# Attention: GpSimd adds layer 0's product to the residual behind its first product of values, and VectorE's statistics follow the score products

## The reference, cut to what matters

```python
x = L0_attn_x
xn = _layernorm(x)
s = _L0_attn_ref(xn, ...)            # recurrence over the tokens, output product, gate, residual
g = _silu(_L0_ffn_ref(xn, ...))
x = x + s * g                        # the add that the change moves
xn = _layernorm(x)                   # its mean and variance are "the statistics"
s = _L1_attn_ref(xn, ...)            # for each position i of dimension 1: a 4 x 4 attention in 16 heads of 16
g = _silu(_L1_ffn_ref(xn, ...))      # mixture of 8 experts
x = x + s * g

# _L1_attn_ref, per position: q, k, v = x @ W.T + b
scores = einsum('ibhd,jbhd->ijbh', q, k) / sqrt(16), causal over the 4 entries
attn = exp(scores - max) / (1 + sum of exp)
out = einsum('ijbh,jbhd->ibhd', attn, v)
```

## Time and profile before

| | |
|---|---|
| median of 3 runs | 1391.9 us (1391.06 to 1392.94) |
| the profiled execution | 1390.86 us, its span 1389.1 us |
| busy over the span | PE 1166.1 us (84%), DVE 1019.9 us (73%), ACT 628.6 us (45%), POOL 629.5 us (45%) |
| attention stage | 263 to 560 us, of it 16 tiles at 16.3 us each |

### The profile page before, as it was taken

One profiled execution on the slowest core, in us unless ns is written; L12 is line 12 of the kernel. 1 busy time (PEld: TensorE's weight loads), 2 busy tenths in 40 slices (PEclk: granted clock), 3 DMA queues, 4 the chain that ended last, 5 costly groups with the idle time before them and its releaser, 6 DMA issues. The chain is left out here.

```text
span 1389.1 us, 22310 instructions
## 1 busy us (share of the span) xinstructions
PE 1166.1 (84%) x7451; PEld 792.1 (57%) x7451; DVE 1019.9 (73%) x1957; ACT 628.6 (45%) x960; POOL 629.5 (45%) x538
## 2 busy tenths in 40 slices
PE   4799999599988993329999989999999998999910
PEld 3565565367666672215756657566576665666610
DVE  6767777768888899966776667766677666776638
ACT  4865555243434441005363554635446354463522
POOL 5600000038877887024455554554645545454430
PEclk9999999799999997559999999999999999999965
DMA  8170000001111111026445464554645545456469
GB/s 337 63 242 1 1 1 1 16 32 32 32 33 32 33 50 59 1 50 142 78 92 115 74 134 83 96 115 70 138 81 97 113 69 132 86 101 108 67 175 349
DMA packets 148958, 122.51 MB, mean 88 GB/s; under 512 B 88400, under 2 KB 133328, under 8 KB 148720
## 3 DMA queue, kind: packets, MB, share of 16 engines
q1 hardware_dynamic: 114912, 83.90, 20.1%
q0 software_dynamic: 25200, 35.85, 16.4%
q10 hardware_dynamic: 8736, 1.33, 0.5%
HBM read 58.91 MB, written 44.30 MB: 74 GB/s over the span
## 5 line engine op out<-in xcount | busy, mean ns | idle before, releaser
L1755 ACT ACTIVATE e_h_all<-e_pH,e_b1c,e_h_scale 128x512 f32<-128x512 f32 x256 | 199.8, 780 | 273.8 <-PE e_pH L1796 273.7
L1539 POOL DMA_INDIRECT e_xg<-xn_rows,e_icol x140 | 162.9, 1163 | 299.6 <-DVE e_icol L1571 266.7
L1810 PE MATMUL e_pY<-e_w_hi,e_h_hi 128*128 128x256 f16 x1024 | 280.3, 274 | 11.5 <-DVE e_w_lo L1630 11.5
L1811 PE MATMUL e_pY<-e_w_lo,e_h_hi 128*128 128x256 f16 x1024 | 279.9, 273 | 0.0
L1812 PE MATMUL e_pY<-e_w_hi,late 128*128 128x256 f16 x1024 | 279.9, 273 | 0.0
L1673 DVE TENSOR_TENSOR late<-e_h_all,e_h_hi 128x512 f16<-128x512 f32 x256 | 177.6, 694 | 96.4 <-ACT e_h_hi L1755 90.4
L1554 POOL DMA_INDIRECT expert_sums<-late,e_dcol x128 | 212.7, 1662 | 53.5 <-issue 33.4
L1794 PE MATMUL e_pH<-e_xT,e_w_hi 128*128 128x512 f16 x512 | 194.8, 380 | 22.5 <-DMA e_xT<-e_xs 15.3
L1795 PE MATMUL e_pH<-e_xT,e_w_hi 128*128 128x512 f16 x512 | 194.8, 380 | 0.0
L1796 PE MATMUL e_pH<-e_xT,e_w_lo 128*128 128x512 f16 x512 | 194.6, 380 | 0.0
L1810 PEld LDWEIGHTS e_pY<-e_w_hi,e_h_hi 128*128 128x128 f16 x1024 | 100.4, 98 | 35.7 <-DVE late L1673 17.0
(11 more groups left out here) (251 smaller groups left out, 2149.8 us busy)
## 6 DMA issues: line engine op xcount, KB each, us to landing
shared<-expert_w SPq DMA_DIRECT2D x18, 1024.0 KB, 6.5
expert_sums<-a_zero SPq DMA_DIRECT2D x10, 1024.0 KB, 11.3
x_st<-x SPq DMA_DIRECT2D x16, 512.0 KB, 9.2
xn_rows<-shared SPq DMA_DIRECT2D x16, 512.0 KB, 3.0
f_ya<-expert_sums SPq DMA_DIRECT2D x16, 512.0 KB, 7.3
out<-x_st SPq DMA_DIRECT2D x8, 1024.0 KB, 8.5
e_xg<-xn_rows,e_icol POOLq DMA_INDIRECT x140
e_xT<-e_xs SPq DMA_TRANSPOSE x136
```

What stands on the lines that cost most here:

```text
L1539: pool.indirect_dma_start(xg[:, q, 0:D + E], None, v.xn3_dram, bass.IndirectOffsetOnAxis(icol[u][:, q:q + 1], axis=0), bounds_check=N - 1, ...
L1755: last = act.activation(dst, pH[h % NPH][:, :], ACT.Relu, bias=b1c[eu][:, h:h + 1], scale=h_scale[eu][:, 0:1])
L1810: pe.matmul(pY[:, q, :], h_hi[:, h, cols], w2_hi[:, h, :], start=(h == 0), stop=False)
L1811: pe.matmul(pY[:, q, :], h_hi[:, h, cols], w2_lo[:, h, :], start=False, stop=False)
```

## The change

For tiles 3 to 15 the add L1046 moves from DVE to POOL: POOL's body t does it for tile t + 3 behind its j = 0 product, after waiting for that tile's L1043. DVE's body for t of 1 or more is split: L1043 (now `finish`) at its head, then the four score products, and only then the statistics (`measure`), which wait for `x1_ready`. Tiles 0, 1 and 2 keep the old order.

```diff
+                        if j == 0 and left >= 3:
+                            pool.wait_ge(op_ready, t + 4)
+                            pool.tensor_tensor(v.x_st[:, :, t + 3, :],
+                                               v.prod_st[:, t + 3, :].rearrange("p (b d) -> p b d", b=B),
+                                               v.x_st[:, :, t + 3, :], ALU.add).then_inc(x1_ready, 1)
                         if j == 1 and left >= 3:
                             scale(t + 3, 1 - u)
...
-                def layer0(t):
+                def finish(t):
                     dve.wait_ge(o_done, t + 1)
                     dve.tensor_tensor(v.prod_st[:, t, :], pX[:, :, :].rearrange("p b d -> p (b d)"),
                                       v.prod_st[:, t, :], ALU.mult).then_inc(op_ready, 1)
-                    dve.wait_ge(op_ready, t + 1)
-                    dve.tensor_tensor(v.x_st[:, :, t, :], v.prod_st[:, t, :].rearrange("p (b d) -> p b d", b=B),
-                                      v.x_st[:, :, t, :], ALU.add).then_inc(x1_ready, 1)
+
+                def measure(t):
                     dve.wait_ge(x1_ready, t + 1)
                     dve.sem_inc(passed, 1)
                     for b in range(B):
                         last = dve.bn_stats(st[:, b, :], v.x_st[:, b, t, :])
...
+                def layer0(t):
+                    finish(t)
+                    dve.wait_ge(op_ready, t + 1)
+                    dve.tensor_tensor(v.x_st[:, :, t, :], v.prod_st[:, t, :].rearrange("p (b d) -> p b d", b=B),
+                                      v.x_st[:, :, t, :], ALU.add).then_inc(x1_ready, 1)
+                    measure(t)
...
                     if left >= 2:
-                        layer0(t + 2)
+                        if t:
+                            finish(t + 2)
+                        else:
+                            layer0(2)
                     dve.wait_ge(k_evac, t + 1)
                     dve.wait_ge(q_evac, t + 1)
...
                     last.then_inc(sm, 1)
+                    if left >= 2 and t:
+                        measure(t + 2)
                     dve.wait_ge(sm, SM * t + 1)
```

More of the change, by code:

```diff
@@ L1053, in layer0 @@
                     dve.wait_ge(bn, t + 1)
-                    if not (isinstance(t, int) and t == 0):
+                    if t:
                         dve.sem_inc(passed, 1)
```

## The result

The changed kernel takes 1425.66 us (median, 1425.14 to 1427.07) beside 1392.42 us of the kernel before: a ratio of 1.0241, 95% interval 1.0223 to 1.0259, slower by 33.2 us. Its profiled execution took 1427.07 us with a span of 1425.3 us, 36.2 us more than the span before; it was the slowest of its four runs. The forecast was 1428.6 us, 37.7 us more than the profiled execution before.

A forecast was written before the change was run, and what follows sets the result against it. PE was taken to bound the kernel at 16.27 us a tile; changed bodies of 18.9 us, 11 periods of 19.2 us and 15.2 us make 245.3 against 207.6 us, so 1390.86 + 37.7 = 1428.6 us, range 1420 to 1436 us.

The forecast's parts named there:

- The bound and the spare: Attention stage before: PE sets 16.27 us a tile; DVE's loop takes 15.9 us, some 0.4 us to spare.
- F: The end of DVE's gated product (L1043) in a tile, from which the prediction counts DVE's chain.
- the way back to F: From the subtraction's end through exponentials, k's evacuation, output matmuls and gated product: 3.97 us without ACT's wait for PE.
- Turns at the port: DVE's four score products alternate with three POOL operations at the shared SBUF port: 8.1 us instead of 2.99.
- POOL's add: The 1024-column add moved to POOL: 2.35 us alone, 2.4 to 3.4 us with its hold-up.
- The subtraction: DVE's L1104 in the changed bodies: gets the port behind POOL's j = 2 sum, ends at F + 15.2.
- rival 1: Port or phases differ: subtraction misses the j = 2 sum (+29 us), add 1.93 us, or POOL operation beside statistics (1409 us); 0.18.
- The sum: Changed bodies, first F to last subtraction: 245.3 us against 207.6 before, +37.7 us, 1428.6 us in all.
- Rival 2: DVE keeps the port through its four back-to-back score products; 1391 us, no change; chance 0.08.
- Rival 3: POOL's add collides with nothing, DVE's loop drops to 13.5 us; up to 5 us faster, 1386 us; chance 0.05.
- Rival 4: With PE waiting 3.4 us per tile its clock is granted at half: +13 us, 1442 us; chance 0.05.
- The sign of 3 us of PE idle before the output matmuls: In the changed profile, PE would stand idle 3 us before output matmuls L1315.

The follow-up runs named there:

- e1: Changed kernel with the four score products multiplying q by a constant in PSUM instead of k in SBUF: 1385.72 us (0.9959 of the kernel before).
- e8: Kernel before with the four score products made as two instructions (12 blocks for 10): 1389.65 us (0.9989 of the kernel before).
- e6: Changed kernel with POOL's scale chain moved from behind j = 1 to behind j = 2: 1416.72 us (1.0177 of the kernel before).
- e2: Kernel before with the score products multiplying q by a constant in PSUM instead of k in SBUF: 1386.17 us (0.9957).
- e3: Changed kernel with the add back on DVE for tiles 3 to 15; statistics still behind the score products: 1411.42 us (1.0140 of the kernel before).
- e4: Changed kernel with POOL's add kept and the statistics back ahead of the score products: 1403.73 us (1.0088 of the kernel before).

## Why the prediction was right

**The bound and the spare.** The prediction gave PE 16.27 us a tile and the chain through DVE 0.4 us to spare. The bound shows in e1: DVE's chain from F to the end of the subtraction takes 9.0 us there, where the changed kernel takes 14.9 and the kernel before 11.9, and the period is 16.30 us like that of before. The spare shows in e8: there this part of the chain takes 12.4 us in the second to sixth body, some 0.5 us more than before, and the period is still 16.30 us. With the 11.89 us that this part took before in the mean, and with the way back to F that took 3.82 us where DVE's chain set the pace (below), the spare comes to 16.30 - 11.89 - 3.82 = 0.6 us, a little more than forecast.

**Turns at the port.** It forecast 8.1 us for the turns, and 0.3 us more where POOL's first product still holds the port at F. The timeline of the changed kernel shows 8.09 to 8.16 us in the four bodies where that product is over at F or within 0.12 us of it, the first among them, and 8.26 to 8.49 us in the other nine. In the body shown the products end at F + 8.2 (428.79 against 420.61) where F + 8.4 was forecast. Idle time of DVE for the add (x1_ready), which would have spoken against the prediction, did not appear.

**POOL's add.** Forecast 2.35 us alone; it is 2.36 us in e1 and 3.3 us with its hold-up, inside the 2.4 to 3.4 us named.

**The subtraction.** Forecast 1.05 us behind the j = 2 sum; it took 1.13 us. Its end stood at F + 15.16 (435.77) for 15.2 in the body shown, and at F + 14.90 in the mean of the 13 bodies (14.63 to 15.16): the forecast had only the first body without POOL's product at F, and there were more. What I named as the first part of rival 1, that it could miss the sum, did not happen; e6 shows its price, 8.9 us, right where 29 against 37.7 us had put it.

**The way back to F.** 3.97 us forecast, 3.82 us measured in the body shown (435.77 to 439.59), as ACT starts k's evacuation 0.09 us before the end of the exponentials when it does not have to wait (436.13 against 436.22). But only six of the twelve ways back took 3.81 to 3.83 us; the others took up to 4.77 us, with slow output matmuls, and the mean is 4.07 us.

**The sum.** From F of the first to the subtraction's end of the last changed body it was 549.72 - 307.11 = 242.6 us, for 245.3 forecast and 207.6 before; these 35.0 us are nearly all of the 36.2 us by which the span grew. So the forecast was 2.7 us too long: 3.6 us too much from F to the subtraction, 0.9 us too little on the ways back. Part of the closeness is luck, as the slow matmuls, which the forecast left out, cost some 1.9 us (below) and made up for terms that were too large.

**The rivals.** Rival 2, DVE keeps the port through its four products, fell with the first timeline. Rival 3, faster, needed free passing of the add; e1 shows that even then the change gives nothing (e1 equals e2). Rival 4 came true in part, below. The sign of 3 us of PE idle before the output matmuls was met in part: 1.4 to 3.1 us, 2.3 us in the mean of the twelve behind the first, since PE was busy longer (15.5 us a tile for 14.62).

## What to carry to other kernels

Before work is moved to POOL, list which of DVE's instructions with two SBUF inputs will then stand beside POOL's, and count the hand-overs: in this kernel four such instructions in a row let in three POOL instructions (5.1 us paid for 5.66 us of POOL work, as forecast) and two let in one, so put long POOL operations beside DVE's reductions and statistics, which ran through here (1.4 and 3.0 us with POOL at work beside them), and not beside its products. Fewer and longer DVE instructions, or shorter POOL ones at the hand-overs, can be worth more than less work (21 us by splitting an add, 30 us by merging products with 20% more columns, both in the changed kernel, which even so stayed behind the kernel before). And an engine relieved off the path gives nothing: here the add on DVE was nearly free, as PE set the pace.

## What the runs showed of the hardware

The granted clock of PE fell in some tiles of the changed kernel, where PE waited longer; I had given this a chance of 0.05 and in the form of all tiles. Output matmuls and stretches of the changed kernel:

```profile
456.03 1.85 PE L1331 MATMUL c_pX<-late,shared 64*128 64x512 f32 x4 [3.11 <-ACT c_work L1275]
...
475.20 1.13 PE L1331 MATMUL c_pX<-late,shared 64*128 64x512 f32 x4 [1.79 <-ACT c_work L1275]
...
494.03 2.08 PE L1331 MATMUL c_pX<-late,shared 64*128 64x512 f32 x4 [3.10 <-ACT c_work L1275]
```

```profile
325.30:343.82 18.52, 15.30 (x84) 11.66 (x84) 17.29 (x22) 5.61 (x9) 14.31 (x13) 0.96 0.10 31
343.82:362.30 18.48, 15.92 (x83) 12.19 (x82) 17.60 (x22) 6.15 (x11) 14.36 (x12) 0.91 0.09 30
```

The same four matmuls take 1.13 us at 2.4 GHz (granted clock 1.00 from 475.20 to 476.30) and 2.08 us at 1.2 GHz (0.50 from 494.10 to 496.10). Of the thirteen, six were longer than 1.13 us (2.08, 1.23, 1.36, 1.85, 2.08 and 1.24 us, 3.1 us too much in sum); five of the six stood behind a wait of 2.7 to 3.1 us, one behind 2.1 us. Another wait of 2.1 us (before 342.65) had its output matmuls at 1.13 us, but slow ones of v behind them, and none was slow behind 1.4 to 1.8 us.

In e3 output matmuls behind waits of 2.07 and 2.70 us took 1.13 us and one group behind 1.93 us took 2.08 us, so that the length of the wait alone does not settle it. Nor did the row that I had set against rival 4: a stretch with PE busy 12.35 of 17 us kept 1.00, and here one with 15.92 of 18.48 us has 0.91. A tile with slow matmuls leaves PE less idle time, and the next one mostly runs at 2.4 GHz again, so the two kinds nearly alternate.

What did the slow clock cost? From one subtraction's end to the next, eight of the twelve distances are 18.82 to 18.85 us and the other four 19.16 to 19.48 us, each of these with slow output matmuls of 1.36 us or more: the cost was some 1.9 us, less than the 3.1 us, in part because POOL's first product is over by a later F and holds the port no more. This is read from the trace; no run took the slow clock away alone. In e4, where PE waits 1.2 to 1.5 us, the clock stayed at 1.00.

The hold-up at the port repeats closely: 3.25 to 3.35 us for POOL's 13 adds, 3316 ns in the mean, and 1.12 to 1.14 us for the subtraction in all 13 changed bodies. What gives the port to one engine when both ask for it was not tried; the timelines here only show the two engines taking turns.
